# The next batch's first layer norm inside the last attention, the inverse sums behind the maxima, and output rows by row group in turn

## What is computed

```python
def _layernorm(x, axis=-1, eps=1e-05):
    m = jnp.mean(x, axis=axis, keepdims=True)
    v = jnp.var(x, axis=axis, keepdims=True)
    return (x - m) / jnp.sqrt(v + eps)
...
x = x + _L1_xattn_ref(_layernorm(x, axis=-1), ctx_1024, ctx_1024, ...)
...
def _L3_ffn_ref(x, Wq, bq, Wk, bk, Wv, bv, Wr, br, Wo, bo):
    ...
    top_vals, top_idx = jax.lax.top_k(dist, K)
    ...
    scores = jnp.einsum('bksd,bktd->bkst', Qk, Kk) / jnp.sqrt(jnp.float32(dh))
    attn = jax.nn.softmax(scores, axis=-1)
    out = jnp.einsum('bkst,bktd->bksd', attn, Vk)
    out = out.transpose(0, 2, 1, 3).reshape(B, S, K * dh)
    return out @ Wo + bo
```

## Time and profile before

| | |
|---|---|
| median of 3 runs | 4084.98 us (4074.66 to 4093.1) |
| the profiled execution's own time | 4093.66 us |
| its span in the profile | 4091.9 us |
| mean granted clock of PE in it | 0.929 of full speed |
| busy: PE, DVE, ACT, POOL | 84%, 56%, 37%, 11% |
| the chain that ended last: PE, DVE, ACT, DMA | 55%, 24%, 8%, 6% |

### The profile page before, as it was taken

How to read it: one execution, slowest core, us unless ns; L and a number is a source line. 1 busy time by engine, 2 the same in 40 slices (tenths; PEclk the granted TensorE clock), 3 DMA queues, 4 the chain that set the end, 5 groups by cost and what they waited for, 6 DMA issues and landing times.

```text
span 4091.9 us, 55117 instructions
## 1 busy us (share of the span) xinstructions
PE 3443.6 (84%) x21294; PEld 1851.1 (45%) x21294; DVE 2301.5 (56%) x5198; ACT 1529.2 (37%) x2358; POOL 432.3 (11%) x323
## 2 busy tenths in 40 slices
PE   7788887787797589998889888898888988889988
PEld 5333333433432378886445324463244543344532
DVE  7664663673664356665643565634657246564356
ACT  5354343434334234443542323523234332254232
POOL 0000000001001134443000020000210001100002
PEclk9899898989989789999999998998998999999989
DMA  7401400410320497775111302113021032201130
GB/s 280 108 10 64 116 10 7 161 22 5 133 53 2 77 264 222 222 228 154 25 27 27 69 6 58 27 25 66 5 53 34 4 38 58 50 15 27 27 69 11
DMA packets 197242, 292.19 MB, mean 71 GB/s; under 512 B 88125, under 2 KB 154319, under 8 KB 180241
## 3 DMA queue, kind: packets, MB, share of 16 engines
q1 hardware_dynamic: 179957, 268.10, 24.8%
q0 software_dynamic: 17024, 20.53, 2.5%
HBM read 210.02 MB, written 77.23 MB: 70 GB/s over the span
## 4 chain that ended last, share of the span: by engine, by line
PE 55%; DVE 24%; ACT 8%; DMA 6%; issue 5%; SPq 1%; POOL 1%; another core or an unknown queue 0%; DVEq 0%; ACTq 0%; POOLq 0%
PE ps L877 6%; DVE max_parts L2097 5%; PE ps L827 5%; PE ps L829 4%; PE ps L828 4%; PE ps L1036 4%; PE ps L1265 3%; PE ps L1272 3%; PE ps L996 3%; PE ps L1158 2%; PE ps L1419 2%; PE ps L1019 2%; DMA q_stack<-in_exp_W 2%; PE ps L1193 2%; ACT arena L1538 2%
## 5 line engine op out<-in xcount | busy, mean ns | idle before, releaser
L877 PE MATMUL ps<-ternary_W,ident 128*128 128x512 f16 x2260 | 677.2, 415 | 134.4 <-ACT arena L1665 40.8
L2097 DVE TENSOR_REDUCE max_parts<-ps 128x1 f32<-128x512 f32 (+3 forms) x768 | 384.4, 551 | 196.4 <-PE ps L999 122.4
L1538 ACT ACTIVATE arena<-ps 128x256 f32<-128x256 f32 (+7 forms) x512 | 318.8, 650 | 447.3 <-PE ps L1019 258.0
L877 PEld LDWEIGHTS ps<-ternary_W,ident 128*128 128x128 f16 x2260 | 226.9, 105 | 454.4 <-issue 152.5
L1848 POOL TENSOR_TENSOR arena<-arena 128x640 f32<-128x640 f32 x96 | 154.9, 1614 | 1999.8 <-ACT arena L1770 1998.6
L2017 DVE CAST arena<-arena 128x256 f16<-128x256 f32 (+2 forms) x424 | 162.0, 382 | 255.0 <-ACT arena L1702 136.0
L1604 ACT ACTIVATE arena<-ps 77x1024 f32<-77x1024 f32 x192 | 190.6, 1017 | 196.7 <-PE ps L1185 194.0
L1770 ACT ACTIVATE arena<-ps 128x1024 f32<-128x1024 f32 x128 | 130.7, 1024 | 335.2 <-PE ps L1408 328.9
L996 PE MATMUL ps<-k_stack,q_stack 96*128 96x512 f16 (+3 forms) x576 | 196.6, 378 | 65.5 <-DVE max_parts L2097 32.8
L2019 DVE TENSOR_TENSOR arena<-arena 128x256 f16<-128x256 f32 (+2 forms) x424 | 241.6, 570 | 14.7
L2532 DVE TENSOR_REDUCE max_parts<-ps 128x1 f32<-128x512 f32 x256 | 166.5, 686 | 143.1 <-PE ps L1392 141.3
(11 more groups left out here) (444 smaller groups left out, 7395.4 us busy)
## 6 DMA issues: line engine op xcount, KB each, us to landing
arena<-scr_expert_weights SPq DMA_DIRECT2D x52, 1024.0 KB
k_stack<-scr_expert_weights SPq DMA_DIRECT2D x26, 1024.0 KB
q_stack<-in_exp_W SPq DMA_DIRECT2D x16, 1024.0 KB
scr_expert_weights<-k_stack SPq DMA_DIRECT2D x16, 1024.0 KB, 4.9
q_stack<-scr_q SPq DMA_DIRECT2D x108, 128.0 KB, 3.8
scr_q<-arena SPq DMA_DIRECT2D x48, 256.0 KB, 2.3
k_stack<-scr_q SPq DMA_DIRECT2D x72, 128.0 KB, 4.7
scr_q<-arena SPq DMA_DIRECT2D x16, 512.0 KB, 4.2
```

The source lines that it names most:

```text
L877: pe.matmul(s[:, 0:CH], ident[:], Wq1[:, 0, 0:CH], start=True, stop=True)
L1538: act.activation(PR[:, n % NP, kt * P:T], slot(L, "ST", g, kt, j)[:, kt * P:T], ACT.Exp).then_inc(*did("act", L, "exp", g, kt, j))
L2097: dve.tensor_reduce(mpart[:, j * NT + t, c:c + 1], slot(L, "S", g, t, j, c)[:, 0:n], AX, ALU.max).then_inc(*frees("dve", L, "S", g, t, j, c))
```

## The change

The diff has five pieces.

1. The steps LN, XN and T of C leave the head of the list. They are now done in the pass before: the statistics and roots of both chunks in F's stage, where DVE waits for the picked heads' weights; the normalised rows (NX) in head 3 at kt = 4 and 5; the transpositions with their copy and lower half (NT) in the tail, chunk 0 between SB(3) and the output projection, chunk 1 behind it. The filler matmuls of T are left out. For batch 0 the same steps stand at the end of phase 1, and the last pass does them for a row that nobody reads.
2. ON(h-1) moves from kt = 3 to kt = 6 for h = 1 and 2, behind the maxima, MT and the padding of keys; for h = 3 to kt = 2.
3. PA also sums tile 7 for heads 0 to 2 (`last_sum`), on DVE and POOL, and SB of these heads is then 4 instructions in place of 8 (2 calls in place of 4).
4. The output projection is done by head, with the matmuls of a tile of rows 0 to 63 and one of rows 64 to 127 in turn, into different banks.
5. SB(3), NT 0, heads 0 to 2, ON(3), head 3, NT 1 is the new order of the tail.

```diff
@@ context_attention (list of the chunks)
-        norm(N, c)
-        add(3.5, "T", N, c)
+        if N != "C":
+            norm(N, c)
+            add(3.5, "T", N, c)
@@ last_attention_steps
-            if h and kt == 3:
+            if h + 1 == HS and kt in (4, 5):
+                steps += [("NX", kt - 4)]
+            if h and kt == (6 if h + 1 < HS else 2):
                 steps += [("ON", h - 1)]
         steps += [("PV", h, NT - 1)]
-    return steps + [("SB", HS - 1), ("WS", 0), ("WS", 1), ("WS", 2), ("ON", HS - 1), ("WB", 0), ("WB", 1), ("WB", 2), ("WL",)]
+        if h + 1 < HS:
+            steps += [("PA", h, NT - 1)]
+    return steps + [("SB", HS - 1), ("NT", 0), ("W", 0), ("W", 1), ("W", 2), ("ON", HS - 1), ("W", 3), ("NT", 1)]
+
+
+def last_sum(h):
+
+    return NT - 1 if h + 1 < HS else NT - 2
@@ PE
-            def head_output(t, h, first, last):
...
-            def last_output_part(kind, h):
...
+            def head_output(h):
+
+                if h == 0:
+                    for p, name in enumerate(("S0", "S1", "B0", "B1")):
+                        banks[p] = claim(name, "F3", "W", p)
+                pe.wait_ge(*of("dve", "F3", "onlo", h))
+                for t in range(TCH):
+                    outs = [banks[(c * TCH + t) // 2][:, t % 2 * D:(t % 2 + 1) * D] for c in range(2)]
+                    for n, (a, b_) in enumerate(((0, 0), (0, 1), (1, 0))):
+                        for c in range(2):
+                            r = slice(DS * c, DS * (c + 1))
+                            mm = pe.matmul(outs[c], ON4[r, a, h, t * P:(t + 1) * P], Wp[r, pi["F3o"], b_, h, :], start=h + n + t % 2 == 0,
+                                           stop=h + 1 == HS and n == 2, skip_group_check=True, tile_position=(DS * c, 0))
+                            if h + 1 == HS and n == 2 and t % 2:
+                                mm.then_inc(*did("pe", "F3", "W", (c * TCH + t) // 2))
                     if h == 0:
...
@@ PE, SB
-                        pe.wait_ge(*of("dve", "F3", "PA", h, NT - 2))
-                        pe.wait_ge(*of("pool", "F3", "PA", h, NT - 2))
-                        for n, p in enumerate((PA4[h % 2], PR4[:, (h * NT + NT - 1) % NP])):
+                        pe.wait_ge(*of("dve", "F3", "PA", h, last_sum(h)))
+                        pe.wait_ge(*of("pool", "F3", "PA", h, last_sum(h)))
+                        parts_of_sum = [PA4[h % 2]] + [PR4[:, (h * NT + kt) % NP] for kt in range(last_sum(h) + 1, NT)]
+                        for n, p in enumerate(parts_of_sum):
@@ end of phase 1 on PE, ACT and DVE (DVE shown)
             experts()
+            dve.wait_ge(*of("ld_next", 0))
+            for c in range(2):
+                chain_step("LN", "C", c)
+            for c in range(2):
+                chain_step("SD", "C", c)
+                chain_step("XN", "C", c)
+            for c in range(2):
+                chain_step("T", "C", c)
             batch_end(dve, "dve")
@@ DVE, the last attention
+                    elif s[0] == "NX":
+                        chain_step("XN", "C", s[1])
...
+                chain_step("T", "C", 0)
                 residual("F3", X, None, X)
+                chain_step("T", "C", 1)
                 dve.memset(rt[0:1, 95:96], 0.0).then_inc(*step("final"))
```

More of the change, by code:

```diff
@@ L1132, in chain_step @@
                     s = claim("A", "T", N, c)
[L1133 removed]
+                    if N != "C":
+                        busy(s, 2 if c else 12)
                     for t in range(TCH):
@@ L1840, in _ @@
                 for h in range(HS):
-                    for kt in range(1, NT - 1):
+                    for kt in range(1, last_sum(h) + 1):
                         pool.wait_ge(*of("act", "F3", "exp", h, kt))
```

58 lines of the change are left out of this document (27 added, 31 removed).

## The result

The changed kernel took 4059.38 us (median of 14 runs, 4049.43 to 4073.93) against 4089.77 for the kernel before on the same chips: a ratio of 0.9928, 95% interval 0.9916 to 0.9941. That is 0.7% faster, 30 us, where the forecast had 55. The profiled execution took 4055.66 us, with a span of 4053.8 and a granted clock of 0.927.

The account below looks back on a forecast made before the run. PE waited for DVE's maxima (40.5 us); PE bound the tail, one chain the pass head. 4 x (-14.0 + 8.4 - 1.9 - 3.3) - 16.5 + 3.8 = -55.9 from 4093.66 gave 4037.8, as median 4030; range 4010 to 4064.

Parts of the forecast that it names:

- the three terms named for it: Upper end of the range, 4064: output pairs not overlapping, POOL slowing ON, and half the gain at a pass's head.
- step 5: Head 3: normalised rows, 2 x 1.38 us on DVE, offset by ON(2) one tile earlier: 0, between -1 and +2.
- ON leaves kt = 3: Heads 1 and 2: PE no longer waits for maxima there, 2 x 6.98 = -14.0 us a pass.
- ON(0) at its new place: Third score of head 2: wait grows to 6.3 us, with 2.44 of slow work: +8.4 us a pass, bounds +4.5 and +11.
- POOL's slowing: Rival: POOL's sums slow ON(0) and head 3's normalised rows on DVE: +10 to +14, time 4042, chance 0.10.
- ON(1) costs nothing: Head 3: ON(1) and two sums end 2.9 us after its first exponential; SB(2)'s halving pays for the wait: 0.
- Output projection: Tail: alternating row groups run side by side, 48 pairs of 0.113 us, with eight transpositions added: -3.3 us a pass.
- the rival without them: Output projection's pairs don't overlap, 10.6 us for 5.4: +5.2 a pass, +21, time 4051, chance 0.10.
- Head of a pass: Passes 2 to 4: 25 matmuls before the first score, 7.5 us for 13.25; taken as -5.5 x 3 = -16.5 us.
- the third rival: Thin cover: statistics show (+14), half the pass-head gain (+8), head 2's stall near its upper bound (+10): time 4061, chance 0.08.
- Batch 0: Ahead of the barrier before the first pass: 9.3 us of moved steps, less 5.5 behind it: +3.8 us, once.
- the slow rival: Clock stays at 0.50 through head 2 after the 6.3 us stall: 90 us in four passes, time 4120, chance 0.03.

Follow-up runs that it names:

- the attention's part alone: The kernel before with every hunk of the change in the last attention and none that moves C's norm: ratio 0.9935 to the kernel before.
- 12 and 12: The changed kernel with a head's 24 output matmuls as all 12 of one row group, then all 12 of the other: ratio 0.9970 to the kernel before.
- three edits: The changed kernel with padding in head 0 and its key load early, normalised rows in the tail, ON(0) and ON(1) in three pieces: 0.9815 to the kernel before.

## Why the prediction was partly wrong

Faster was right, and so was most of the mechanism, but the gain was 30 us for 55: 4059 us measured for 4030. That is inside the range, near an upper end (4064) which was meant for things that mostly didn't happen; the three terms named for it add up to some 40 us above 4030 and not 34. The step that failed is step 5, the normalised rows put at nothing. By its steps:

1. *ON leaves kt = 3*: no wait for maxima is left at kt = 4. Head 1 fell by 7.4 us, for 8.0. Right.
2. *ON(0) at its new place*: a wait of 7.13 us for 6.3, and slow work behind it. Right in kind, 0.8 short (1.1 in passes 2 to 4), because I took the padding at 3.62 us where it now takes 4.66, at a place where POOL has its sums. I had put POOL's slowing into a rival and priced only ON and the rows by it. The run with ON back at kt = 3 shows what else stands there: the padding and the added sum alone already make a wait of 2.36 us. Head 2 is 1.9 us longer than before, for 0.4.
3. *ON(1) costs nothing*: nearly right. In passes 2 to 4 the second of the two sums behind ON(1) takes 1.70 us beside POOL's, for 0.55, and ends 4.0 us behind head 3's first exponential, for my 2.9; PE waits 1.9 us there, ahead of SB(2). With the rows out of head 3 (the attention's part alone) SB(3) comes at 17.6 us in pass 1 and 18.7 in the others, for 18.3 before: +0.2 a pass.
4. *SB halved*: 1.01 us to the next start for 1.87, so 0.86 saved in each of heads 1 and 2, for 0.97.
5. *Normalised rows cost nothing*: here the prediction failed. I wrote that "ON(2) now stands one tile earlier, which buys about as much as this costs". ON(2) does start earlier, by 2.4 us in pass 1 and 1.3 in the others. But five sums stand behind it for four (5.6 to 6.7 us for 3.8 without the rows between them), so at SB(3) the earlier start had bought 0.7 us in pass 1 and nothing in passes 2 to 4, as under 3. The rows were then paid in full, also where POOL's sums stretched the first of them from 1.37 to as much as 3.90 us: PE waits 1.7 to 3.2 us ahead of SB(3) for 1.2. Forecast 0, between -1 and +2; measured +2.8 us a pass with step 3. Three runs that take the rows out of head 3 give 2.4 to 2.7 of it back.
6. *Output projection*: the pairs came at 0.057 us a matmul as forecast, and the rival without them priced a thing that didn't happen; the run with 12 and 12, which takes away only part of the overlap, lost 12 to 17 us of its 21. But the projection starts behind a wait, and in two passes of four SB(3) or the transpositions run partly at 1.2 GHz: -2.8 for -4.1. I had taken both at the times of rows at full clock.
7. *Statistics hidden*: right. The wait that hides them has 0.95 us left of 4.36.
8. *Head of a pass*: 9.4 us for 7.5. 12 matmuls at the low clock were right (13 now); the pause of 1.2 to 1.8 us, PE's instructions coming late, was not in any row that I read. It is a term that I left out; only the third rival had room for it.
9. *Batch 0*: +3.2 for +3.8. The terms that I listed make 9.9 us and not 9.3, so +4.4 by them.

The missing 28 us are thus head 3 (11), the tail's slow clock (5), head 2 (6), the head of a pass (4) and head 1 (2), less 1 at the start. The rivals: POOL's slowing came in part, at the padding and at the rows, and not at ON(0), whose cast kept its 0.43 us. The time of the thin cover, 4061, was met by luck: of its 32 us the statistics' 14 did not come, and head 3, which it doesn't name, made up for most of them. The clock was back at 1.00 behind the first 4.2 us after the long wait, so the slow rival fell.

The two rules of the Trainium skill. By "TensorE: Matmul & The Clock Gate", section "LDWEIGHTS (loading the stationary operand)", a load of 128 columns costs about 107 ns. The trace has 92 to 95 ns for each load of the last 72 matmuls, not far from it:

```profile
L967 PEld LDWEIGHTS ps<-weights_padded,arena x72: 92/94/95, 2979.4 to 2983.1; 64*128 64x128 f16 x72
```

What the trace speaks against is my reading that a pair costs two loads one after the other: all 72 matmuls and their loads fit into 4.10 us, so loads of the two row groups lie side by side. "GPSIMD Engine Reference", section "Specifications", on the shared SBUF interfaces, agrees with the padding: 4.73 us beside POOL's sums, and 2.93 in the runs that had it in head 0, before POOL's first sum.

## What to carry to other kernels

An instruction moved up in an engine's order starts earlier only as far as what it waits for allows, and what then stands behind it can take the gain back: count the gain at the next wait of the engine that you feed, not at the start of the instruction. On an engine that feeds another, work is free only where a row shows that engine idle and the next wait is not its own; here 2.8 us of DVE work cost 5 us in a head with maxima, some 3.6 in the head with sums only (2.6 there and a slow SB(3) behind it) and nothing in the tail. A wait that leaves TensorE idle for some microseconds is paid twice, by itself and by slow work behind it, so remove the last piece of it too: by the stretches, three edits worth 43 us apart gave 53 together.

## What the runs showed of the hardware that was not expected

- The same instructions take different times from pass to pass through the granted clock. Between the first score and the first exponential, with 1941 matmuls in each, PE was busy 347.74 us in pass 2 before and 342.30 after, and the stretch took 400.03 and 392.09. At one place, 2526 to 2530 us, unchanged code ran at a clock of 0.67 before and 1.00 after. With the attention's part alone, whose middle is the old kernel's, the stretch took 398.84, 392.71, 398.64 and 393.01. With ON back at kt = 3, whose middle is the changed kernel's, its mean was 397.4 for 394.0. So a difference of 4 us in such a stretch can't be put down to an edit.

```profile
2475.44:2875.47 400.03, 347.74 (x1941) 187.34 (x1940) 198.13 (x481) 151.18 (x186) 0.00 (x0) 0.94 0.22 40
```

```profile
2475.46:2867.55 392.09, 342.30 (x1941) 185.34 (x1940) 201.63 (x499) 151.61 (x189) 0.00 (x0) 0.95 0.22 41
```

- Fillers right behind a restart don't pay here: on top of the three edits the granted clock of PE's first 5.0 us in passes 2 to 4 was 0.50, 0.66 and 0.63 with them and 0.50, 0.50 and 0.70 without, and real work in their place brought the first score 1.3 to 3.4 us forward.
- Bulk loads can hold up an engine's own instructions. After a restart of a changed kernel PE paused 0.7 to 3.0 us behind its first 13 matmuls while 1.5 MB of loads kept the DMA engines 71 to 89% busy, until 1.2 to 1.6 us after a 16 KB block of instructions had landed, and not when the loads came later. The profile calls such a pause "issue" and names no releaser; the packets of the instruction queue tell what it was.
